# Attention scores from two exact float32r parts per value, two heads at once in the halves of the rows; the causal mask added by a product

## The reference

```python
x = x + 0.5 * _L0_ffn_ref(_layernorm(x), ...)      # 8 experts of width 512, one per token
x = x + _L0_attn_ref(_layernorm(x), Wq, Wk, Wv, Wo)
x = x + 0.5 * _L0_ffn_ref(_layernorm(x), ...)
```

```python
q, k, v = (split_heads(x @ W.T) for W in (Wq, Wk, Wv))
q, k = _rope(q, pos), _rope(k, pos)
score = jnp.einsum('bqd,bkd->bqk', q, k)
score = jnp.where(causal[None], score, -jnp.inf)
attn = jax.nn.softmax(score / jnp.sqrt(8.0), axis=-1)
out = jnp.einsum('bqk,bkd->bqd', attn, v)
```

## Time and profile before

| | us |
|---|---|
| time, median of 3 runs (908.14, 914.18, 915.40) | 914.18 |
| span of the profiled execution | 855.6 |
| attention in it, 202 to 714 | 512 |
| of it stages with all kinds of work, 250 to 688 | 438 |
| period of one such stage (400.24 to 430.54) | 30.3 |

### The profile page before, as it was taken

The page is one execution under the profiler, slowest core; times in us unless marked ns, Lnnn a source line. Parts: engine busy times, 40 slices in busy tenths (PEclk is TensorE's granted clock), DMA queues, the critical chain, the costliest instruction groups (busy, mean ns, idle before and its releaser), DMA issues. The chain is left out here.

```text
span 855.6 us, 17846 instructions
## 1 busy us (share of the span) xinstructions
PE 779.7 (91%) x5570; PEld 427.9 (50%) x5570; DVE 610.9 (71%) x1919; ACT 507.4 (59%) x1229; POOL 315.4 (37%) x603
## 2 busy tenths in 40 slices
PE   9889999887899999999999999999999997689995
PEld 8888896543233333333333333333333335579884
DVE  4657774698668777788878878788787722856663
ACT  2166651673247767667667766766777684146662
POOL 6177742475104223223322422331242231056753
PEclk8699999998569999999999999999999998789998
DMA  8721113065332033033113303312320001122110
GB/s 271 270 57 50 54 33 117 23 169 159 57 57 45 14 57 57 10 49 58 34 26 57 53 6 57 58 22 36 57 41 18 3 1 34 73 70 50 52 42 26
DMA packets 27989, 51.84 MB, mean 61 GB/s; under 512 B 7552, under 2 KB 19200, under 8 KB 26496
## 3 DMA queue, kind: packets, MB, share of 16 engines
q1 hardware_dynamic: 21296, 41.04, 20.7%
q0 software_dynamic: 4096, 8.69, 3.8%
q10 hardware_dynamic: 2512, 1.06, 0.5%
HBM read 35.40 MB, written 14.97 MB: 59 GB/s over the span
## 5 line engine op out<-in xcount | busy, mean ns | idle before, releaser
L1448 DVE CUSTOM_DVE_ANT_0 cst<-psS,mask_row 128x768 bf16<-128x768 f32 (+7 forms) x512 | 364.7, 756 | 100.2 <-PE psS L1308 97.6
L1412 ACT ACTIVATE prob<-psST 128x512 f32<-128x512 f32 (+3 forms) x750 | 317.3, 495 | 158.9 <-PE psST L1339 155.2
L1353 PE MATMUL a_psO<-prob,vs 128*32 128x512 f32 (+3 forms) x1536 | 166.7, 506 | 2.8 <-ACT prob L1412 1.7
L1532 POOL TENSOR_TENSOR a_gate<-a_zeros 1x1 f32<-1x1 f32 x128 | 23.7, 185 | 333.7 <-ACT prob L1412 333.7
L1339 PE MATMUL psST<-a_qs,ks 75*128 75x512 bf16 (+1 forms) x480 | 123.7, 327 | 5.9 <-ACT prob L1412 3.5
L1308 PE MATMUL psS<-ks,a_qs 72*128 72x512 bf16 (+2 forms) x480 | 119.0, 337 | 5.6 <-DVE a_rowmax L1448 5.5
L777 POOL DMA_INDIRECT tok<-rows,f_there_number x64 | 61.8, 966 | 86.0 <-DVE f_number L489 42.0
L1308 PEld LDWEIGHTS psS<-ks,a_qs 72*128 72x128 bf16 x480 | 35.6, 99 | 101.1 <-DVE a_rowmax L1448 33.0
L1308 PE MATMUL psS<-ks,qs 72*128 72x512 bf16 (+3 forms) x288 | 75.8, 354 | 6.7 <-DVE a_rowmax L1448 6.5
L1533 POOL TENSOR_SCALAR_AFFINE_SELECT prob<-prob 128x512 f32<-128x512 f32 x128 | 80.3, 627 | 0.0
L1339 PE MATMUL psST<-qs,ks 75*128 75x512 bf16 (+3 forms) x270 | 73.4, 346 | 2.7 <-ACT prob L1412 1.7
(11 more groups left out here) (183 smaller groups left out, 1066.1 us busy)
## 6 DMA issues: line engine op xcount, KB each, us to landing
a_qs<-q_split SPq DMA_DIRECT2D x60, 96.0 KB
rows<-tok SPq DMA_DIRECT2D x8, 536.0 KB, 4.9
ks<-k_split SPq DMA_DIRECT2D x32, 128.0 KB
qs<-q_split SPq DMA_DIRECT2D x36, 96.0 KB
q_split<-p_part SPq DMA_DIRECT2D x24, 128.0 KB, 2.4
k_split<-p_part SPq DMA_DIRECT2D x24, 128.0 KB, 2.4
ks<-k_split SPq DMA_DIRECT2D x16, 192.0 KB
tok<-x_after_first SPq DMA_DIRECT2D x4, 536.0 KB, 5.4
```

The lines of the kernel that those rows point to most:

```text
L1353: last = nc.tensor.matmul(psO[32 * h:32 * h + 32, c0:c0 + w], vs[r][:, j, h, :], prob[:, u % RING, h, 0:w], start=(j == 0), stop=(u + 1 in ...
L1412: nc.scalar.activation(prob[:, u % RING, h, 0:w], score_buffer(s, u * QH + h)[:, 0:w], ACT.Exp, scale=SCALE).then_inc(exp_done, 1)
L1448: last = nc.vector.tensor_tensor_reduce(out=out[:, a * CH:a * CH + width], in0=ps[:, a * CH:a * CH + width], in1=mask_row[:, S - width:], ...
```

## The change

**Parts.** A value x is split into two float32 numbers: `high`, x with its low 12 bits cleared (a shift right and left on the integer view, VectorE), and `low = x - high` (VectorE). Both have at most 12 significant bits and are stored as float32, and the products take them as float32r. The stack of a head is 2 x 2 x 8 = 32 rows, one constant row (unused rows are zero or -1), and for the scores two more constant and three maximum rows, 37 in all. Stacks are float32: 4 bytes a value where there were 2.

**Two heads at once.** Even heads have their rows at partitions 0 to 36, odd heads at 64 to 100. Two products of a pair are issued one after the other, one on each half of TensorE's rows, into different PSUM banks.

**Mask.** VectorE no longer adds the mask. For tiles on the diagonal a further bf16 product, the identity against a mask of 128 columns for each head, accumulates the mask into PSUM, and VectorE takes a plain `reduce_max` of two or four heads in one instruction. Query tiles 4 to 7 are cut in two: the keys 0 to 511 without a mask, and the rest with it; a small `combine` on VectorE joins the two maxima.

**Buffers.** The scores have two buffers of two banks (one pair each); exp reads a pair in one instruction. The maxima have one buffer X of two banks and one buffer Y of one bank (for single heads and the small transposes), used in turn. So 4 + 2 + 1 + 1 banks.

**Other.** ScalarE has no casts left in the projection, GpSimd only the sum; GpSimd sets constant rows (8 instructions at the start, 4 behind the projection). The stack is loaded by 12 transfers as against 11, and the maxima by two transfers a half as against one.

The core of the diff:

```diff
-KINDS = 3
-PR = KINDS * KINDS * DK
-MR = KINDS
+KINDS = 2
+LOW_BITS = 12
+PAIRED = KINDS * KINDS * DK
+PR = PAIRED + 1
+MAX_ROW = PAIRED + 2
+MAX_KINDS = 3
+FR = MAX_ROW + MAX_KINDS
...
-        n.psST = [ctx.enter_context(nc.psum_tensor(f"psST{i}", [P, CH], F32)) for i in range(3)]
-        n.psS = [ctx.enter_context(nc.psum_tensor(f"psS{i}", [P, 2 * CH], F32)) for i in range(2)]
+        n.psST = [ctx.enter_context(nc.psum_tensor(f"psST{i}", [P, 2 * CH], F32)) for i in range(2)]
+        n.psX = ctx.enter_context(nc.psum_tensor("psX", [P, 2 * CH], F32))
+        n.psY = ctx.enter_context(nc.psum_tensor("psY", [P, CH], F32))
...
+        def split(g, k):
+
+            for i in range(2):
+                dve.wait_ge(summed[i], g + 1)
+                wait(dve, split_stored[i][k], 16 * KINDS * (g // 2))
+                nc.vector.tensor_scalar(high[i][k][:, :].bitcast(I32), rot[i][k].bitcast(I32), LOW_BITS, LOW_BITS,
+                                        ALU.logical_shift_right, ALU.logical_shift_left).then_inc(hi_done[i], 1)
             for i in range(2):
                 dve.wait_ge(hi_done[i], g + 1)
+                nc.vector.tensor_tensor(low[i][k], rot[i][k], high[i][k][:, :], ALU.subtract).then_inc(lo_done[i], 1)
...
+    def ending(half):
+
+        i0 = half * CB
+        two = [("two", i0 + k, 2 * p, half * CH, (k + 1) * P, True) for k in (3, 2) for p in range(PAIRS)]
+        return two + [("four", i0 + k, 0, half * CH, (k + 1) * P, True) for k in (1, 0)]
+
+    full_pairs = [("two", i, h, 0, CH, False) for i, h in ((CB, 0), (CB, 2), (CB + 1, 0))]
+    full_ones = [("one", i, h, 0, CH, False) for i in (TB - 1, TB - 2) for h in range(QH)]
+    full_ones += [("one", CB + 1, h, 0, CH, False) for h in (2, 3)]
...
+            def maxima(there, h, start, stop):
+                at = side(h)
+                return nc.tensor.matmul(there, qs[r][at:at + PR, q_col(h, i * P):q_col(h, i * P) + P],
+                                        ks[r][at:at + PR, h // 2 * S + c0:h // 2 * S + c0 + w], start=start, stop=stop)
...
+            if masks:
+                mask = n.mask[:, :].unsqueeze(1).to_broadcast([P, count, P])
+                for b in range(2):
+                    there = ps[:, b * CH:b * CH + count * w].rearrange("p (a c) -> p a c", a=count)[:, :, w - P:]
+                    last = nc.tensor.matmul(there, n.identb[:, :], mask, start=False, stop=True)
             last.then_inc(use_done, 1)
...
-            nc.tensor.matmul(score_buffer(s, m)[:, 0:w], ks[r][:, h * S + j * P:h * S + (j + 1) * P],
-                             qs[r][:, q_col(h, q0):q_col(h, q0) + w], start=True, stop=True).then_inc(scored, 1)
+            for h in (2 * p, 2 * p + 1):
+                at = side(h)
+                last = nc.tensor.matmul(score_buffer(s, m)[:, h % 2 * CH:h % 2 * CH + w],
+                                        ks[r][at:at + FR, h // 2 * S + j * P:h // 2 * S + (j + 1) * P],
+                                        qs[r][at:at + FR, q_col(h, q0):q_col(h, q0) + w], start=True, stop=True)
+            last.then_inc(scored, 1)
...
+                nc.scalar.activation(prob[:, u % RING, 2 * p:2 * p + 2, 0:w],
+                                     score_buffer(s, m)[:, :].rearrange("p (a c) -> p a c", a=2)[:, :, 0:w], ACT.Exp,
...
-                last = nc.vector.tensor_tensor_reduce(
-                    out=out[:, a * CH:a * CH + width], in0=ps[:, a * CH:a * CH + width], in1=mask_row[:, S - width:],
-                    scale=1.0, scalar=LOWEST, op0=ALU.add, op1=ALU.max, accum_out=rowmax[:, h, i:i + 1])
+            nc.vector.reduce_max(there, of, AX.X).then_inc(use_read, 1)
...
+            nc.vector.tensor_tensor(rowboth[:, :, :], rowmax[:, s % 2, :, CB:], rowfull[:, s % 2, :, :],
+                                    ALU.max).then_inc(combined, 1)
```

More of the change, by code:

```diff
@@ L8 @@
 F32 = mybir.dt.float32
+F32R = mybir.dt.float32r
 BF16 = mybir.dt.bfloat16
@@ new lines, in columns, with use_cost, score_cost @@
+    def columns(t):
+        return t[4] * {"one": 1, "two": 2, "four": 4}[t[0]]
+    tile_order, left = [], {"X": list(wide), "Y": list(narrow)}
+    while left["X"] or left["Y"]:
+        want = "X" if not tile_order or tile_order[-1][0] == "one" else "Y"
+        tile_order.append(left[want if left[want] else "XY".replace(want, "")].pop(0))
+    def use_cost(t):
+        return columns(t) + 70
+    tile_total = sum(use_cost(t) for t in tile_order)
+    def score_cost(u):
+        return units[u][3]
@@ L1168, in plan, with is_use, uses, buffer_of @@
         return found
-    OPEN, OPEN_AFTER, OPEN_TILES = CB, 4, 3
+    def is_use(what):
+        return what in ("tile", "turn_max", "turn_out")
+    def uses(first, last):
+        return [(what, arg, buf) for what, arg, _, buf in plan(first, last) if is_use(what)]
+    def buffer_of(t):
+        return "Y" if t[0] == "one" else "X"
+    first_half = max(k for k, t in enumerate(tile_order) if half_of(t) == 0) + 1
+    before_loop = [("tile", t, buffer_of(t)) for t in tile_order[:first_half]] + [("turn_max", 0, "Y")]
@@ L1206, in q_col, with maxima_known, side @@
+    def maxima_known(s, half):
+        start, found = (0, before_loop) if s == 0 else (base[s - 1], stage_uses[s - 1])
+        return start + 1 + max(k for k, (what, arg, _) in enumerate(found) if what == "tile" and half_of(arg) == half)
     def q_col(h, q):
-        return (q // CH * QH + h) * CH + q % CH
+        return (q // CH * PAIRS + h // 2) * CH + q % CH
+    def side(h):
+        return h % 2 * HALF
     def sb(name, shape, dt=F32):
         return ctx.enter_context(nc.sbuf_tensor(f"a_{name}", shape, dt))
-    def psum(name, width):
-        return ctx.enter_context(nc.psum_tensor(f"a_{name}", [P, width], F32))
@@ L1486, in _, with do @@
-        for k, (_, what, arg) in enumerate(before_loop):
-            do(-1, what, arg, k, psS[k % 2])
-        run(stage)
-        end = base(NST - 1, False) + len(uses(False, True))
-        normalise(NST - 1, 1, end, psS[end % 2])
+        def do(s, found, start):
+            seen = set()
+            for k, (what, arg, _) in enumerate(found):
+                if what == "tile":
+                    reduce(s + 1, arg, start + k, half_of(arg) not in seen)
+                    seen.add(half_of(arg))
+                    if start + k + 1 == maxima_known(s + 1, 1):
+                        combine(s + 1)
+                elif what == "turn_max":
+                    copy_max(s if arg else s + 1, arg, start + k)
+                else:
+                    normalise(s - 1 if arg else s, arg, start + k)
```

480 lines of the change are left out of this document (236 added, 244 removed).

## The result

The changed kernel takes **1252.8 us** (median of 4 runs, 1249.6 to 1255.5) where the kernel before takes 911.2 (4 runs, 906.6 to 915.4): ratio 1.376, 95% interval 1.369 to 1.382. The forecast was 880, range 852 to 950. The profiled execution took 1249.6 us with a span of 1247.8: only 1.8 us lie outside the span, and 1.7 in the repeated profile of the kernel before (914.6 and 912.9). The forecast's gain is a difference of spans, so it does not hang on this.

A forecast was written before the change was run, and what follows sets the result against it. TensorE was taken to bound the attention stages: 28.1 us a stage instead of 30.3 gave -32, projection -4, opening +3, last stage -1, together -34 against 914.2, so 880 us, range 852 to 950.

The forecast's parts named there:

- The change on TensorE, at full rate: Attention stages: float32r column priced as bf16, two halves as one; TensorE's work 23.6 us a stage, 3.8 less than before.
- TensorE would wait 16% of the time: Attention stages: waiting named as what could make the granted clock of 1.00 fall and the forecast wrong.
- four cycles a column at about 1,200: Rival for float32r products at the whole float32 price: a stage of 50 us, kernel about 1,200; chance 0.06.
- TensorE's work of 23.6 in a stage: Attention stage: scores 3.84, maxima 4.9, mask products 1.7, entering them 1.2, weighted sums 10.6, transposes 1.4 us.
- the second drain: Mask products in a stage: 0.10 us on leaving as well as entering each would add 1.2 us; not in the sum.
- The wait for X: Attention stage: TensorE waits until VectorE has read the single maxima buffer, 4.5 us of 28.1, against 2.9 waiting before.
- Column at one cycle, halves side by side: Scores and maxima: a float32r column costs a bf16 one, two halves cost one; a dense 512-column pair takes 0.21 us.
- Loads exposed: Rival in scores and maxima: 0.10 us per weight load limits pairs below 512 columns; stage 30.3, about 912 us; chance 0.13.
- halves in sequence or two a column: Sign for two rivals: a dense 512-column pair at 0.43 us; kernel 926 (chance 0.06) or 958 us (chance 0.08).
- Projection: Projection, bound by VectorE: 5.45 us a group instead of 5.96, eight groups, 4 us gained.
- the opening: First stage's maxima, at a clock near 1.2 GHz: single X puts TensorE's writes between VectorE's reads; 3 us lost.
- The added constant rows: GpSimd's settings at the start and behind the projection: cost nothing; if uncovered, TensorE would wait for `zeroed`.

The follow-up runs named there:

- pad_small: Changed kernel with each half's products reading 61 (maxima) and 64 (scores) rows instead of 33 and 37, added query-side rows holding 2^-12; 987.1 us.
- before_again: The kernel before, unchanged, profiled once more; span 912.9 us.
- pad_zero: Changed kernel with each half's products reading 61 (maxima) and 64 (scores) rows instead of 33 and 37, added query-side rows holding 0.0; 991.5 us.
- pad_bf16: Changed kernel with rows filled to 61 and 64 of each half, and operands of scores and maxima taken from a constant bfloat16 table; 946.4 us.
- one_side: Changed kernel with the odd heads' products read from the even heads' half of the rows, so no two can overlap; 1473.8 us.
- pad_one_side: Changed kernel with rows filled to 61 and 64, and both heads of a pair read from the first half of the rows; 1461.4 us.

## Why the prediction was wrong, step by step

**The step that failed** is the condition under the whole sum: "The change on TensorE, at full rate", the 1.00 of the earlier trace rows carried into stages whose products read 33 and 37 rows. I named the clock as what would make the forecast wrong, but looked for it in waiting ("TensorE would wait 16% of the time"). It was the other way round: the changed kernel at 97% busy was granted 0.51, the filled one at 90% busy 1.00. The Trainium skill (TensorE: Matmul & The Clock Gate, Part 1: The HAM clock gate) says that activity releases the throttle and idle time brings it back, a gate driven by how busy TensorE is; by that rule both kernels would be at 1.00 and the changed one the likelier. The profile disagrees: the busy share did not tell the level here, and the rows that the products read moved it. None of my rivals held this; the nearest in time, four cycles a column at about 1,200, came close for the wrong reason.

Sizes: from the changed kernel to pad_small the span falls by 262 us (1247.8 to 985.4), and 72.5 stay to before_again's 912.9. Of those, 13 steady periods of 34.05 for 30.3 are 49; the first two (49.9 and 47.1 against 40.3 and 30.3) are 26, and all the rest together gives 3 back.

**TensorE's work of 23.6 in a stage** was mis-sized, at 1.00 too. The waits of TensorE in pad_zero's twin pad_small from 400 to 700 us:

```profile
PE psX L1324 <- DVE a_rowfull L1493: 13.6, 18, 1.1
PE psX L1324 <- DVE a_rowmax L1493: 12.8, 26, 0.7
PE psST L1371 <- ACT prob L1449: 3.0, 9, 0.3
```

29.4 in 300 us are 3.3 a stage, so the work is 34.05 - 3.3 = 30.7. In pad_bf16 the waits are 40.7 in 300, 4.3 a stage, and the work 27.2. Of the 7.1 above the forecast, 3.5 go with float32r (30.7 - 27.2). The other 3.6 were put at nothing, and the rows name most of them:

- Leaving a mask product costs as much as entering one: 128 columns for each of two banks take 0.21 (607.91 to 608.12) for 0.107 of columns, up to twelve times 0.11, 1.3 in all. It has the size of the second drain, which the prediction priced at 1.2 and left out of its sum.
- The small transposes are products of all rows too. The old kernel's stage of 30.7 us with 48 and 64 rows, against 30.3 with 65 and more, puts the cost of going in and out of them at about 0.4; this is an estimate.
- The profile counts a wait only from a product's end, 0.17 behind its columns. With 87 waits in 300 us, 9.1 a stage, up to 1.6 of what is called work here is waiting (an estimate, from the 0.17 of the earlier trace rows).

**The wait for X** was forecast at 4.5. The waits for X alone are 30.8 in 300 us in pad_bf16, 3.2 a stage, and with 0.17 for each of the five up to 4.1; in pad_small 26.4, 3.0 a stage, behind the slower work. This part of the model was about right.

**Column at one cycle, halves side by side**: right, by one_side and by the two pairs in 0.60 (at 1.2 GHz already 1.05 for 1.71).

**Loads exposed** was given 0.13 and a stage of 30.3. At full clock it is the true case, and worse than priced: I let the loads bite in pairs below 512 columns only, but they add 0.11 to the pair of 512 too (0.34 for 0.23), and 0.43 ahead of a mask product. And 0.43 is what I had written down as the sign of "halves in sequence or two a column": the sign didn't single out a case. The Trainium skill (TensorE: Matmul & The Clock Gate, Weight-path perf modes) says that fast weight load is not used for FP32; it does not name float32r, and here a float32r load took 184 ns against 94 in bfloat16, so the trace goes with the rule and against my forecast. I knew the rule and the row of 0.10, and let "loads can run under the other half's columns" outweigh them without a row that showed it.

**Projection**: 5.45 a group forecast. Starts of its products in the changed kernel:

```profile
201.37 3.67 PE L963 MATMUL psST<-p_anT,wall 128*128 128x512 f32 x8
206.82 3.67 PE L963 MATMUL psST<-p_anT,wall 128*128 128x512 f32 x8 [0.42 <-DVE prob L919]
212.27 3.67 PE L963 MATMUL psST<-p_anT,wall 128*128 128x512 f32 x8 [0.41 <-DVE prob L919]
```

5.45, but by luck in part: it was a choice between the bounds 4.8 and 5.9, and two shifts take 1.86 (202.34 to the subtractions at 204.20) where I had 1.2, two subtractions 1.20, the low end of theirs. From the first group's start to the eighth's it is 38.8 us against 41.9 before, a gain of 3.1 for the forecast 4. From there to the first sum it is 40.9 against 35.1: the opening costs 5.8 by then, for the forecast 3. Inside it stands a wait that I had not listed, TensorE idle 5.58 us up to the second tile in X, behind VectorE's last splits:

```profile
228.60 0.49 PE L1324 MATMUL psX<-ks,qs 33*128 33x512 f32 x2
229.03 0.29 PE L1339 MATMUL psX<-mask,identb 128*128 128x128 bf16 x2
...
235.31 0.79 PE L1324 MATMUL psX<-ks,qs 33*128 33x512 f32 x2 [5.58 <-DVE a_rowmax L1493]
236.04 0.40 PE L1339 MATMUL psX<-mask,identb 128*128 128x128 bf16 x2
```

The same pair takes 0.43 ahead of this wait and 0.73 behind it: the clock falls here. The filled kernels have such a wait too (3.81 us in pad_small) and come back, so it is not what keeps the stages low.

**The added constant rows** I cost at nothing, naming only a wait for `zeroed`. That wait is not seen, but the work may have another price, below.

## What to carry to other kernels

Before a product is made narrower in rows, ask what clock it will be granted: here, halving the rows of a TensorE-bound stage cost more than it saved, at 97% busy, and rows that hold zeros were worth reading. Where the granted clock is carried over from another kernel, it is a term of the forecast like a duration, with its own rival. Products in halves save columns, not weight loads: with 4-byte operands price each group by its loads, wide ones too. And price both ways of every change between products of half and of all rows.

## What the runs showed of the hardware

- The granted clock depends on the rows read: in the old kernel's stages, of one order, 1.00 for good after one stage with 72 and 75 rows, after two or three with 64 and 65, after five with 48, and not for good with 37. In the changed kernel, rows of zeros count like rows of 2^-12 (991.5 and 987.1 us, 1252.8 without them).
- A float32r load of 64 x 128 weights takes 184 ns on average against 94 in bfloat16, at the 2.4 GHz level (400 to 700 us). The stage of filled rows is 34.05 us in float32r and 31.5 in bfloat16.
- Between products of half the rows and of all rows, TensorE loses 0.09 to 0.11 us each way (pad_bf16: 0.32 for 0.23 ahead of a mask product, 0.21 for 0.107 behind one).
- Integer shifts on VectorE take longer while an instruction of GpSimd runs. In the changed kernel's projection and behind it, VectorE and GpSimd:

```profile
202.34 1.93 DVE L927 TENSOR_SCALAR p_high<-prob 128x512 int32<-128x512 int32 x2
...
224.35 3.54 DVE L927 TENSOR_SCALAR p_high<-prob 128x512 int32<-128x512 int32 x2
...
229.01 2.93 DVE L927 TENSOR_SCALAR p_high<-prob 128x512 int32<-128x512 int32 x2
```

```profile
201.30 2.69 POOL L1027 TENSOR_TENSOR prob<-prob 128x512 f32<-128x512 f32 x2 [2.77 <-DVE prob L919]
...
225.71 7.98 POOL L1598 MEMSET a_qs<- 2x2048 f32 x4
```

  Two shifts take 1.9 us in the projection, and 3.5 and 2.9 where the four memsets run beside them. Singly the 16 shifts take 0.42 to 2.10 us. Of the pair at 202.34 the second starts at 202.78 and takes 1.49, until 0.28 behind the end of GpSimd's two sums at 203.99; the one at 225.79, beside the first memset, takes 2.10. The Trainium skill (SBUF — State Buffer, SBUF: two separate sides) tells of a port pair that GpSimd and some forms of VectorE instruction hold in turn, each for a whole instruction. The rows fit that, while the two subtractions between the shifts take 1.27 us beside the memsets and 1.28 in the projection. But no run took GpSimd's work away, so it is argued and not shown.

What stays open is what exactly sets the level. The number of rows moves it with all else unchanged, and pad_one_side against pad_small shows that the rows of a product are not the only thing; no run takes that apart further.
